# A decoder layer with eight experts: batches 1 to 3 sorted by expert into 13 tiles of 256 rows by indexed writes, batch 0 dense in front of them

## What is computed

```python
scores = jnp.einsum('bsd,de->bse', x, Wr) + br
_, topk_idx = jax.lax.top_k(scores, K)                   # K = 2 of E = 8
indicator = jax.nn.one_hot(topk_idx, E).sum(-2)
weights = jax.nn.softmax(jnp.where(indicator > 0, scores, neg_inf), axis=-1)
for i in range(E):
    xi = x * indicator[..., i:i + 1]
    h = jax.nn.relu(jnp.einsum('bsd,dh->bsh', xi, W1[i]) + b1[i])     # 128 -> 512
    yi = jnp.einsum('bsh,hd->bsd', h, W2[i]) + b2[i]                  # 512 -> 128
    out = out + yi * weights[..., i:i + 1]
```

## Time and profile before

| | |
|---|---|
| median of 3 runs | 324.56 us (324.31 to 325.76) |
| the profiled execution | 326.34 us, its span 324.6 us |
| TensorE busy | 297.8 us, 1869 matmuls |
| VectorE busy | 206.5 us |
| ScalarE busy | 193.0 us |
| GpSimd busy | 97.8 us |
| DMA | 14.06 MB, mean 43 GB/s |
| mean granted TensorE clock | 0.989 |

### The profile page before, as it was taken

How to read it: one execution, slowest core, us unless ns; L and a number is a source line. 1 busy time by engine, 2 the same in 40 slices (tenths; PEclk the granted TensorE clock), 3 DMA queues, 4 the chain that set the end, 5 groups by cost and what they waited for, 6 DMA issues and landing times.

```text
span 324.6 us, 5407 instructions
## 1 busy us (share of the span) xinstructions
PE 297.8 (92%) x1869; PEld 210.2 (65%) x1869; DVE 206.5 (64%) x444; ACT 193.0 (59%) x525; POOL 97.8 (30%) x140
## 2 busy tenths in 40 slices
PE   6789999999989899797989788889999999999995
PEld 2578677877777568453745343436778878678883
DVE  3767657375548885966376673536686867666652
ACT  1569858387747664466276668867655465354451
POOL 7990190035020200720056152055558110000000
PEclk9799999999999999999999999979999999999999
DMA  8900015530100010001084491000000000100001
GB/s 234 210 3 3 1 23 65 67 43 16 36 0 2 16 35 2 5 0 45 5 253 141 112 280 55 3 0 2 0 1 2 0 0 0 35 0 0 2 1 32
DMA packets 14889, 14.06 MB, mean 43 GB/s; under 512 B 2620, under 2 KB 10892, under 8 KB 14860
## 3 DMA queue, kind: packets, MB, share of 16 engines
q1 hardware_dynamic: 13278, 12.92, 16.4%
q10 hardware_dynamic: 1584, 0.80, 0.9%
HBM read 9.94 MB, written 0.52 MB: 32 GB/s over the span
## 4 chain that ended last, share of the span: by engine, by line
PE 73%; DVE 13%; ACT 3%; DMA 3%; issue 3%; SPq 2%; POOL 1%; DVEq 0%; ACTq 0%; POOLq 0%
PE ps L663 7%; PE ps L665 7%; PE ps L664 7%; PE ps L737 6%; PE ps L770 5%; PE ps L782 4%; PE ps L944 4%; PE ps L945 4%; PE ps L946 4%; DVE mneg L1306 4%; PE ps L815 3%; PE ps L852 3%; PE ps L744 2%; SPq L412 2%; DMA w_in<-in_L_attn_W_qkv 2%
## 5 line engine op out<-in xcount | busy, mean ns | idle before, releaser
L1062 ACT ACTIVATE p<-ps,negmax 128x256 f32<-128x256 f32 (+1 forms) x128 | 52.7, 426 | 25.2 <-DVE negmax L1277 24.7
L1392 DVE SCALAR_TENSOR_TENSOR hid_lo<-ps,hid_hi 128x512 fp32r<-128x512 f32 x64 | 43.6, 688 | 33.7 <-ACT hid_hi L1126 33.4
L1306 DVE TENSOR_REDUCE mneg<-ps 128x2 f32<-128x512 f32 x64 | 42.5, 684 | 18.6 <-PE ps L815 18.5
L1126 ACT ACTIVATE hid_hi<-ps 128x512 fp32r<-128x512 f32 x64 | 37.5, 598 | 26.8 <-PE ps L665 26.7
L1092 ACT ACTIVATE px<-ps 128x512 f32<-128x512 f32 x64 | 36.1, 598 | 17.8 <-PE ps L837 17.5
L1277 DVE TENSOR_REDUCE negmax<-ps 128x2 f32<-128x512 f32 (+1 forms) x48 | 32.9, 686 | 19.6 <-PE ps L739 12.5
L815 PE MATMUL ps<-k_st,q_mem 128*128 128x256 bf16 x128 | 24.7, 276 | 9.0 <-DVE mneg L1306 7.6
L504 POOL TENSOR_SCALAR tmp<-mv 128x2 f32<-128x2 f32 x8 | 1.9, 233 | 95.3 <-DVE mv L1301 95.3
L1048 ACT CAST t_hi<-ps 128x512 fp32r<-128x512 f32 x32 | 18.8, 592 | 19.5 <-PE ps L665 18.6
L663 PE MATMUL ps<-x_hi,w_hi 128*128 128x512 f32 x64 | 25.6, 400 | 1.7 <-issue 1.5
L1062 ACT ACTIVATION_READ_ACCUMULATOR p<-ps,negmax 128x1 f32 x128 | 26.6, 208 | 0.0
(11 more groups left out here) (184 smaller groups left out, 663.7 us busy)
## 6 DMA issues: line engine op xcount, KB each, us to landing
w_raw<-in_L_ffn_W SPq DMA_DIRECT2D x2, 1024.0 KB, 6.1
w_last<-in_L_ffn_W SPq DMA_DIRECT2D x8, 256.0 KB, 6.1
k_st<-k_part SPq DMA_DIRECT2D x12, 128.0 KB
q_mem<-q_part SPq DMA_DIRECT2D x48, 32.0 KB
w_in<-in_L_attn_W_qkv ACTq DMA_DIRECT2D x2, 384.0 KB, 6.3
w_in<-in_L_attn_W_qkv SPq DMA_DIRECT2D x2, 384.0 KB, 7.1
resid<-in_x SPq DMA_DIRECT2D x2, 256.0 KB, 4.0
p<-in_L_attn_W_o SPq DMA_DIRECT2D x1, 512.0 KB, 8.3
```

What stands on the lines that cost most here:

```text
L1062: last = act.activation(dst, bank[:, n * i:n * i + n], ACT.Exp, bias=negmax[:, kt, h:h + 1], accum_out=psums[:, kt, h:h + 1])
L1126: act.activation(hid[0][:, c, :], ps[:, hidden_banks[NC * k + c], :], ACT.Relu).then_inc(s_ha, 1)
L1306: dve.tensor_reduce(mneg[:, qt, :].rearrange("p (r g) -> p r g", r=2)[:, :, g], ps[:, max_bank[("MX", b, u)], :].rearrange("p (h k) -> p h ...
L1392: dve.scalar_tensor_tensor(hid[1][:, c, :], ps[:, hidden_banks[NC * k + c], :], 0.0, hid[0][:, c, :].bitcast(F32), ALU.max, ALU.subtract). ...
```

## The change

Batch 0 (256 rows) goes densely through eight experts as before, with passes of 256 rows. The 768 rows of batches 1 to 3 are sorted. Each row is written twice (once for each chosen expert) as a line of 132 numbers, with its pair number, into a table `xs` in DRAM by indexed DMAs of GpSimd (`dispatch`, 12 writes of 128 lines). The places are worked out on the chip: one-hot choices, cumulative counts by triangular fp32 matmuls on TensorE (unit PS, `ranks`), and arithmetic on VectorE (`places`), once for blocks 2 to 5 and once for blocks 6 and 7. Expert e owns tile e of 256 lines; what does not fit goes to one of five spare tiles. So there are always 8 + 5 = 13 tiles, and empty places hold padding that is written to `xs` early. VectorE also works out which expert each spare tile belongs to (unit OV, `spares`).

SyncE reads the table back in three parts (`xr`), and TensorE turns the lines (two tiles at a time, unit X). A pass is now 256 rows: two units H and two units Y, each of two blocks of 256 columns side by side in a bank. For a spare tile the weights come from `ovw`, two buffers that SyncE fills from the split weights by four DMAs at an address read from `spare_i` (`spare_weights`). ScalarE adds the bias of the second layer (unit E, `tile_out`), TensorE turns the tile (YT), VectorE copies it (`rows_out`), and GpSimd writes it by pair number into `ys` in DRAM (`collect`, 26 writes). In the end SyncE reads `ys` back in three parts, and VectorE adds each row's two lines, times their gates (`add_pairs`, 12 operations).

In the cross-attention slots the weight casts, GpSimd's order and the router of batch 0 move. All 32 slots of cross-attention now stand ahead of the first expert slot; before, the last two slots of the last batch stood in the first expert slots.

```diff
+DT, ST = TPB, NT - TPB
+PAIRS = 2 * ST * P
+CAP = 256
+SPARE = PAIRS // (CAP + 1)
+NS = NE + SPARE
+ROW = D + 4
+FIRST = 8
+SEQ = tuple([("D", e) for e in range(FIRST)] + [("S", j) for j in range(NS)] + [("D", e) for e in range(FIRST, NE)])
+ROUTED = ((0, DT), (DT, NT - TPB), (NT - TPB, NT))
...
-            more = {(1, 6): [("WS", 0, 0)], (2, 1): [("WS", 0, 1)], (2, 5): [("WS", 0, 2)], (2, 6): [("NT", 0)],
-                    (2, 7): [("RT", 0)], (3, 0): [("EX", 0)], (3, 0.5): [("GT", 0)], (3, 2): [("W2", 0, 0)],
-                    (3, 3): [("WT", 0), ("WS", 0, 3)], (3, 4): [("X", 0)]}
+            more = {(0, 7): [("WS", 0, 0)], (1, 0): [("WS", 0, 1)], (1, 1): [("WS", 0, 2)], (1, 3): [("WS", 0, 3)],
+                    (1, 5): [("WS", 0, 4)], (1, 7): [("BT", 0)], (2, 1): [("WS", 0, 5), ("NT", 0)],
+                    (2, 2): [("RT", 0)], (2, 3): [("WS", 0, 6), ("EX", 0)], (2, 4): [("GT", 0), ("WS", 0, 7)],
+                    (2, 5): [("W2", 0, 0)], (2, 6): [("W2", 0, 1), ("WT", 0)], (2, 7): [("W2", 0, 2)],
+                    (3, 0): [("W2", 0, 3), ("X", 0)], (3, 1): [("W2", 0, 4)], (3, 2): [("XC", 1)],
+                    (3, 6): [("NT", 1), ("XC", 2)], (3, 7): [("RT", 1)]}
...
+        beside = {(0, 0, "h"): [("PS", 1), ("CO", last, 3)], (0, 1, "h"): [("oq0", last), ("W2", 0, 5)],
+                  (1, 0, "y"): [("oq1", last)], (1, 0, "h"): [("oT0", last)], (1, 1, "y"): [("oT1", last)],
+                  (1, 1, "h"): [("wo", last), ("W2", 0, 6)], (2, 0, "h"): [("EX", 1)], (2, 1, "h"): [("W2", 0, 7), ("GS", 1)],
+                  (3, 0, "h"): [("NT", 2), ("XC", 3)], (3, 1, "y"): [("RT", 2)], (4, 1, "y"): [("PS", 2)],
+                  (5, 0, "h"): [("EX", 2)], (5, 1, "h"): [("GS", 2), ("OV", 0)]}
...
+            slot = [("X", x) for x, tiles in enumerate(x_units) if x and tiles[0] == i + 1]
+            for u in range(2):
+                if i:
+                    slot += [("Y", i - 1, u)]
...
+                    if u == 1 and kind == "S":
+                        slot += [("E", j)]
+                    if u == 0 and i >= 2 and SEQ[i - 2][0] == "S":
+                        slot += [("YT", SEQ[i - 2][1])]
+                slot += beside.get((i, u, "y"), [])
+                if i < len(SEQ):
+                    slot += [("H", i, u)]
+                slot += beside.get((i, u, "h"), [])
...
+            sp.wait_ge(s_xs, 16 * 2 * ST)
+            for i, (n0, n1) in enumerate(XR_PARTS):
+                sp.dma_start(xr[:, 2 * n0:2 * n1, :], xs.rearrange("(n p) d -> p n d", p=P)[:, 2 * n0:2 * n1, :]
+                             ).then_inc(s_xr[i], 16)
+
+            def spare_weights(o):
+
+                if o >= 2:
+                    sp.wait_ge(s_y, 2 * SEQ.index(("S", NE + o - 2)) + 2)
+                e = sp.value_load(spare_i[0:1, o:o + 1], min_val=0, max_val=NE - 1)
+                for k, w in enumerate((w1_hi, w1_lo, w2_hi, w2_lo)):
+                    sp.dma_start(ovw[:, o % 2, k, :].bitcast(F32), w[:, bass.ds(e * HID, HID)].bitcast(F32)
+                                 ).then_inc(s_ovw[o % 2], 16)
...
+            for n in range(2):
+                sp.wait_ge(s_ys[n], 32 * len(range(n, NS, 2)))
+            for b in range(1, B):
+                ns = slice(2 * TPB * (b - 1), 2 * TPB * b)
+                sp.dma_start(yg[:, ns, :], ys.rearrange("(n p) d -> p n d", p=P)[:, ns, :]
+                             ).then_inc(s_yg[b - 1], 16)
...
+            def collect(j):
+
+                pool.wait_ge(s_misc_ev, misc_at[("YT", j)] + 1)
+                for h in range(2):
+                    pool.indirect_dma_start(ys, bass.IndirectOffsetOnAxis(xr[:, 2 * j + h, D:D + 1].bitcast(U32), 0),
+                                            yrow[:, j % 2, P * h:P * h + P], None, bounds_check=PAIRS - 1,
+                                            oob_is_err=False).then_inc(s_ys[j % 2], 16)
...
             norm_3(2)
+            second_weights(4)
+            first_low(7)
+            second_weights(5)
+            pool.wait_ge(s_init, 16)
+            late = [(t, c) for t in range(*ROUTED[1]) for c in range(2)]
+            for t, c in late[:3]:
+                dispatch(t, c)
             norm_3(3)
+            for t, c in late[3:]:
+                dispatch(t, c)
+            second_weights(6)
+            second_weights(7)
+            for t in range(*ROUTED[2]):
+                for c in range(2):
+                    dispatch(t, c)
+            for j in range(NS):
+                collect(j)
...
+                if u == 0:
+                    if kind == "D" or j < NE:
+                        pe.wait_ge(s_wlo, j + 1)
+                    else:
+                        pe.wait_ge(s_ovw[j % 2], 64 * ((j - NE) // 2 + 1))
+                    pe.wait_ge(s_xlo, x + 1)
```

More of the change, by code:

```diff
@@ L300, in decoder_layer @@
[L300 to L312 removed]
+                slots.append(slot)
@@ new lines, in decoder_layer @@
+        x_units, i = [], 0
+        while i < len(SEQ):
+            n = 2 if SEQ[i + 1:i + 2] and SEQ[i + 1][0] == SEQ[i][0] else 1
+            x_units.append(tuple(range(i, i + n)))
+            i += n
+        x_of = {i: (x, h) for x, tiles in enumerate(x_units) for h, i in enumerate(tiles)}
+        x_kind = [SEQ[tiles[0]][0] for tiles in x_units]
+        beside = {(0, 0, "h"): [("PS", 1), ("CO", last, 3)], (0, 1, "h"): [("oq0", last), ("W2", 0, 5)],
[3 more added lines that the diff above has]
+                  (5, 0, "h"): [("EX", 2)], (5, 1, "h"): [("GS", 2), ("OV", 0)]}
@@ new lines, in rows_in @@
+            def rows_in(x):
+                if x == 0:
+                    pe.wait_ge(s_mx_ev, 16 * B)
+                    pe.wait_ge(s_misc_ev, misc_at[("WT", 0)] + 1)
+                elif x_kind[x - 1] == "D":
+                    pe.wait_ge(s_xf, x_kind[:x].count("D"))
+                else:
+                    pe.wait_ge(s_xlo, x)
+                for n, i in enumerate(x_units[x]):
+                    kind, j = SEQ[i]
+                    if kind == "D":
+                        last = pe.matmul(ps[:, X_BANK, CAP * n:CAP * n + CAP], pick[:, j, :], wgtT[:, :], start=True, stop=True)
+                    else:
+                        pe.wait_ge(s_xr[next(q for q, (n0, n1) in enumerate(XR_PARTS) if j < n1)], 16)
+                        for h in range(2):
+                            c0 = CAP * n + P * h
+                            last = pe.transpose(ps[:, X_BANK, c0:c0 + P], xr[:, 2 * j + h, 0:D], ident[:, :])
+                last.then_inc(s_gt, 1)
@@ L948, in second_bias @@
-            def second_bias(hf):
-                pe.wait_ge(s_b2, 32)
-                pe.matmul(ps[:, Y_BANK[hf], :], b2_sb[:, :], wgtT[:, 512 * hf:512 * hf + 512].bitcast(F32),
-                          start=False, stop=False)
+                for n in range(2):
+                    c = slice(P * (2 * u + n), P * (2 * u + n) + P)
+                    if kind == "D" or j < NE:
+                        w = [w[:, j, c] for w in w1_p]
+                    else:
+                        w = [ovw[:, j % 2, k, c] for k in range(2)]
+                    last = products(ps[:, bank, CAP * n:CAP * n + CAP], w,
+                                    [part[:, x % 2, CAP * half_x:CAP * half_x + CAP] for part in x_p])
@@ L953, in _, with second_bias @@
+            def second_bias():
+                pe.matmul(ps[:, Y_BANK["D"], 0:CAP], b2_sb[:, :], wgtT[:, :].bitcast(F32), start=False, stop=False)
             for at, slot in enumerate(slots):
```

577 lines of the change are left out of this document (389 added, 188 removed).

## The result

| | before | after |
|---|---|---|
| median | 325.16 us of 4 | 354.9 us of 4 |
| ratio of the runs compared | | 1.0903, 95% interval 1.0844 to 1.0961 |
| profiled execution, its span | 326.34, 324.6 us | 355.28, 353.5 us |
| TensorE busy | 297.8 us | 285.1 us |
| VectorE, ScalarE, GpSimd busy | 206.5, 193.0, 97.8 us | 198.0, 183.4, 137.4 us |

What follows compares the result with a forecast made beforehand. It took TensorE's streamed columns to bound the kernel before, and waits in queues after. Start 223.5, dense 39.3, sorted 47.4, spare waits 17.1, clock 4 and tail 15 made 346.3 us; forecast 346, range 329 to 364.

Steps and rivals of the forecast that it cites:

- What bounds, what is taken away: Expert stage: TensorE's streamed columns set the time; 256-column matmuls at 0.12 us take 27.8 us off.
- Start 223.5: End of cross-attention: first expert tile starts at 223.5 us, not 214.6, after held casts and all last-batch slots.
- The hold by the fourth cast: Cross batch 1: fourth first-layer cast waits for a late last-row load, ends at 187.0, holding exponentials 9.5 us.
- Dense tiles 39.3: Eight dense tiles: 39.3 us, from VectorE's in-order queue and a 4 us TensorE wait for sorted rows.
- Sorted tiles 3.5 each: Thirteen sorted tiles: 3.5 us each plus 1.9 for the last combine, 47.4 us in all.
- term 2: Dense tiles, 39.3 us: includes a 1.6 to 1.7 us chain through ScalarE and VectorE against 1.44 us of slack.
- Spare waits 17.1 and clock 4: Last three spare tiles: reload cycles of 7.5 us cost 17.1 (low end 5.6, 11.4); low clock after holes, 4 us.
- Tail 15: After the last combine: bias, turn, two index writes, landing, read back, adds and output take 15 us.
- The rival that the columns decide: Expert stage: TensorE stays the bound, VectorE's runs fit the slack, reloads are short; 312 us, chance 0.10.
- the one with both waits small: Spare-weight waits and clock loss both drop out, the rest as forecast; 325 us, no change, chance 0.05.
- The slow rate for spare weights: Spare tiles: SBUF-to-SBUF loads at the slow rate, 12.6 us more; 359 us, chance 0.15.
- 2.4 us an index write: GpSimd sets the pace: each index write takes 2.4 us, rows land 11 us later; 370 us, chance 0.12.

Runs made afterwards that it cites:

- e6: Changed kernel with spare tiles placed between owned ones (341.44 us), plus counts of blocks 2 to 5 moved behind the last batch's output steps: 338.22 us.
- e4: Changed kernel with VectorE's arithmetic for places and spare tiles left out, using constant places and experts: 351.75 us.
- e12: e10 with combines three halves behind, spare tiles and gates worked out during the wait, adds in six parts, bf16 counts, 15 idle matmuls: 329.62 us.
- e1: Changed kernel with the last three spare-weight reloads left out, so those tiles run on stale weights: 341.55 us.
- e9: e5 with batches 0 to 2 sorted and batch 3 dense, run behind the 13 sorted tiles: 342.1 us.
- e5: Changed kernel with spare tiles between owned ones (341.44 us), plus a five-place last-row ring, five loads ahead of stacking, earlier first bias: 336.83 us.
- e10: e9 with units moved to where their input is ready, and 20 idle matmuls while TensorE waits for the rows: 335.26 us.
- e8: Changed kernel with spare tiles between owned ones, the edits of e5 and e6, and the eighth dense tile last: 334.36 us.

## Why the prediction was right, and where not

**What bounds, what is taken away: right.** A 256-column matmul costs 0.12 us, TensorE is busy 12.7 us less, and that decides nothing.

**1. Start 223.5: measured 230.35, 6.9 too early.** The hold by the fourth cast was right, to 0.8 us. The three stretches behind it were each too short. The next four slots took 10.4 us where 7.5 was forecast: they had taken 9.8 before (177.96 to 187.74, not "about 12"), and nothing came back. Batch 2 took 18.5, forecast 16: it had taken 16.2 before (not 14). Batch 3 took 15.2, forecast 13: "six took 9.8 us, 203.93 to 213.72" is a miscount, since the exponentials at 213.72 are those of the sixth slot. Five slots took 9.8 us, 1.96 each, and eight at that rate are 15.7.

**2. Dense tiles 39.3: measured 46.6 (230.35 to 276.96), the term that was most off.** VectorE in order and the wait for the rows were right. Mis-sized: the counts. They were priced by the router's matmuls as 2.9 us of TensorE's work for both rounds. The first round alone is 1.5 us of waiting for the choice and 2.8 of products, and the low clock there nearly doubles the 1.07 us of the product with the values. e6 gave 3.2 us of it back, e4 3.1 for the places behind it.

**3. Sorted tiles 3.5 each: measured 3.44.** e12 gives a combine more slack, and there TensorE is busy in 35.98 us of 256 to 292. Yet its pairs are turned 6.8 to 7.2 us apart where no router step stands between, against 6.9 in the changed kernel. So 3.4 to 3.5 is TensorE's own time here, not the chain through ScalarE and VectorE as term 2 had it.

**4 and 5. Spare waits 17.1 and clock 4: the mechanism was right, both sizes were not.** The spare stage holds 14.5 us of them (61.1 us from slot 8 to the last combine, less 46.6), and e1 gave 13.4 back. TensorE stands 8.0 us, not 17.1: the cycle was 5.1 to 5.7 us, not 7.5, and at the low clock the work between release and first use took 3.2 and 2.8 us, not 1.66. The low end of 5.6 was the better row. By the formula of the Trainium skill (DMA: Bandwidth & Descriptors, Anatomy of one DMA), which stands there for DMAs issued by GpSimd, the waits would have been 12; the 8.0 us lie below it too. The clock, on the other hand, was put at 4 us for the whole kernel. Here alone it costs some 5.5 us, an estimate: 12.5 us in which matmuls start every 0.21 instead of 0.12 us. The same estimate gives 3 us at the first dense tile and 1.3 behind the first sorted rows, which term 2 had to bear.

**Tail 15: measured 15.4.** Its largest piece was mis-split: an index write holds GpSimd 1.28 us as taken, but four stand there, not two.

The errors of +6.9, +7.3, -0.8, -6.6 and +0.4 make +7.2, which is span 353.5 against 346.3. That the sum came so near is partly luck: two terms together 14.2 us too small were half offset by the spare stage, 7.4 too large, and inside it waits put too high by 9 hid a clock put too low. The other 1.7 of the 8.9 us between 346 and the median is nearly all that the profiled execution of before stood 1.8 above the median to which the difference was added. The rival that the columns decide (312 us) is out, and so is the one with both waits small (325): they were 8.0 and 3.39 us. The slow rate for spare weights and 2.4 us an index write are out by the landings and by 0.98 us.

## What to carry to other kernels

Fewer columns are worth nothing until the rows are there in time: lay out the path from the last input to the first tile, and from the last tile to the output, and put the work that needs neither beside them. Sorting the batches that are ready first, with the last one dense and last, removed the tail (15.4 to 3.7 us), but the choice and the writes then have to fit into the stage before. By itself it did not pay: e9 (342.1 us) was slower than e5 (336.8), and e10 (335.3), with its units moved, no faster than e8 (334.4) in the old order; e12's edits, which gave 329.6, were not tried in that order. A reload costs nothing behind four tiles of other work and 2 to 4 us without. And a hole on TensorE can be paid a second time in the clock: behind those of 3.77, 1.91 and 2.28 us at the spare tiles matmuls came to start 0.21 us apart, behind the one of 2.27 us at 262.92 they kept 0.12.
